# Running the second matmul of a stacked half tile over all 128 rows

## The reference

```python
e = jnp.stack([tbl_0[ids[:, 0]], ..., tbl_38[ids[:, 38]]], axis=1)     # (512, 39, 16)
x0, xk = e, e
for idx, (W, b) in enumerate(params):           # three layers, 128 outputs each
    z = jnp.einsum('bhd,bkd,hks->bsd', x0, xk, W) + b[None, :, None]
    z = jax.nn.relu(z)
    if idx != n_layers - 1:
        xk = z[:, :64, :]
        direct.append(z[:, 64:, :])
    else:
        direct.append(z)
logit = jnp.sum(jnp.concatenate(direct, axis=1), axis=-1)
h = jnp.maximum(jnp.concatenate([logit, dense_ctx], axis=1) @ W_top1 + b_top1, 0.0)
h = jnp.maximum(h @ W_top2 + b_top2, 0.0)
y = h @ W_top3
```

## Time and profile before

| | |
|---|---|
| median of three runs | 661.69 us (661.02 to 662.9) |
| profiled execution | 662.2 us |
| span of its trace | 660.4 us |
| TensorE matmul busy | 623.2 us, 94% |
| VectorE busy | 576.9 us, 87% |
| GpSimd busy | 464.8 us, 70% |
| ScalarE busy | 283.8 us, 43% |
| matmuls at L522 | 32, mean 497 ns |

### The profile page before, as it was taken

The page is one execution under the profiler, slowest core; times in us unless marked ns, Lnnn a source line. Parts: engine busy times, 40 slices in busy tenths (PEclk is TensorE's granted clock), DMA queues, the critical chain, the costliest instruction groups (busy, mean ns, idle before and its releaser), DMA issues.

```text
span 660.4 us, 7186 instructions
## 1 busy us (share of the span) xinstructions
PE 623.2 (94%) x1916; PEld 357.3 (54%) x1916; DVE 576.9 (87%) x507; ACT 283.8 (43%) x341; POOL 464.8 (70%) x277
## 2 busy tenths in 40 slices
PE   0359999999999999999999999999999999999998
PEld 0125555555656555555655555555656555555553
DVE  3358899999999999999999999999999999999670
ACT  2123554444344554444344554444344554444223
POOL 6609877786869877786869877786869877706240
PEclk9998999999999999999999999999999999999999
DMA  6789796877949395967949395967949394962000
GB/s 228 168 201 207 148 211 143 191 148 157 194 109 218 69 223 103 202 136 162 190 109 214 70 222 107 201 137 158 194 111 216 75 227 95 201 132 68 2 0 0
DMA packets 28511, 98.20 MB, mean 149 GB/s; under 512 B 8081, under 2 KB 17041, under 8 KB 20434
## 3 DMA queue, kind: packets, MB, share of 16 engines
q1 hardware_dynamic: 21267, 93.54, 64.1%
q0 software_dynamic: 5120, 1.32, 2.0%
q10 hardware_dynamic: 2111, 3.20, 1.4%
HBM read 94.20 MB, written 3.84 MB: 148 GB/s over the span
## 4 chain that ended last, share of the span: by engine, by line
PE 86%; DVE 5%; issue 4%; ACT 1%; DMA 1%; POOL 1%; SPq 1%; DVEq 0%; POOLq 0%; ACTq 0%
PE z L528 40%; PE z L539 13%; PE z L534 12%; PE z L536 11%; PE z L519 4%; DVE products L406 4%; PE z L522 2%; DMA x_rep<-x_rows 1%; POOL low L309 1%; PE z L521 1%; PE spare L573 1%; PE z L597 1%; DVE low L309 1%; PE xk L597 1%; ACT xk L623 1%
## 5 line engine op out<-in xcount | busy, mean ns | idle before, releaser
L406 DVE TENSOR_TENSOR products<-x_rep,xk 128x1024 f32<-128x1024 f32 (+1 forms) x288 | 366.6, 1333 | 25.5 <-ACT xk L623 25.1
L309 POOL TENSOR_TENSOR low<-products,high 128x1024 fp32r<-128x1024 f32 x112 | 264.9, 2390 | 125.3 <-ACT high L639 83.9
L528 PE MATMUL z<-products,w_whole 128*128 128x512 f32 x672 | 311.2, 595 | 0.0
L639 ACT ACTIVATE high<-products 128x1024 fp32r<-128x1024 f32 x176 | 184.3, 1056 | 237.6 <-DVE products L406 180.5
L362 POOL DMA_INDIRECT gathered<-in_tables,rows_sb x160 | 199.1, 1245 | 46.5 <-issue 44.4
L534 PE MATMUL z<-high,w_high 128*128 128x512 f32 x352 | 187.9, 534 | 10.0 <-ACT high L639 10.0
L528 PEld LDWEIGHTS z<-products,w_whole 128*128 128x128 f32 x672 | 128.1, 191 | 112.0 <-issue 99.1
L536 PE MATMUL z<-high,w_low 128*128 128x512 f32 x352 | 139.7, 397 | 0.0
L539 PE MATMUL z<-low,w_high 128*128 128x512 f32 x352 | 113.9, 405 | 3.0 <-DVE low L309 2.3
L534 PEld LDWEIGHTS z<-high,w_high 128*128 128x128 f32 x352 | 66.8, 190 | 55.5 <-issue 32.9
L309 DVE TENSOR_TENSOR low<-products,high 128x1024 fp32r<-128x1024 f32 x64 | 94.2, 1473 | 1.1 <-ACT high L639 1.1
(11 more groups left out here) (34 smaller groups left out, 102.5 us busy)
## 6 DMA issues: line engine op xcount, KB each, us to landing
x_rep<-x_rows SPq DMA_DIRECT2D x60, 768.0 KB
x_rep<-x_rows SPq DMA_DIRECT2D x62, 512.0 KB, 6.4
x_rows<-gathered SPq DMA_DIRECT2D x15, 225.0 KB
x_rep<-x_rows SPq DMA_DIRECT2D x8, 384.0 KB, 16.0
x_rep<-in_w ACTq DMA_DIRECT2D x2, 1280.0 KB
gathered<-in_tables,rows_sb POOLq DMA_INDIRECT x160
x_same<-x_rows SPq DMA_DIRECT2D x15, 90.0 KB
x_same<-x_rows SPq DMA_DIRECT2D x15, 78.0 KB
```

Of the source, the lines that this page charges most:

```text
L309: ops.tensor_tensor(low[0:p, slot, 0:n, :], products[0:p, index % RING, 0:n, :], high[0:p, slot, 0:n, :].bitcast(fp32), ALU.subtract).then ...
L406: nc.vector.tensor_tensor(slots, rep, row.unsqueeze(1).broadcast_to([p, n, N]), ALU.mult).then_inc(made, 1 + pair)
L528: mm = nc.tensor.matmul(out, w_whole[0:p, at, i, :], products[0:p, slot, i, :], start=(t + i == 0), stop=(t + i == tiles[layer] - 1))
L639: nc.scalar.activation(high[0:p, slot, 0:n, :], products[0:p, index % RING, 0:n, :], ACT.Copy).then_inc(rounded, 1)
```

## The change

The second matmul of a stacked half tile (L522) multiplies all 128 rows of `stacks` by the low part of the weights, where it multiplied rows 0 to 63 before. `w_stack_low` has 128 partitions, with the low part of the same weights in both halves. So the sum gets one more term, the low part of the products by the low part of the weights. The two set-up subtractions (L499) run over 128 partitions.

```diff
-        w_stack_low = sb("w_stack_low", [HALF, len(STACKS), S], fp32r)
+        w_stack_low = sb("w_stack_low", [S, len(STACKS), S], fp32r)
...
-                nc.vector.tensor_tensor(w_stack_low[:, at, :], w_sb[layer][0:HALF, t + 1, :],
-                                        w_stack_high[0:HALF, at, :].bitcast(fp32), ALU.subtract) \
+                nc.vector.tensor_tensor(w_stack_low[:, at, :], w_sb[layer][:, t + 1, :],
+                                        w_stack_high[:, at, :].bitcast(fp32), ALU.subtract) \
                     .then_inc(w_stack_made, 1)
...
-                    mm = nc.tensor.matmul(out, w_stack_low[:, stack, :], stacks[0:HALF, stack, :],
+                    mm = nc.tensor.matmul(out, w_stack_low[:, stack, :], stacks[:, stack, :],
                                           start=False, stop=True)
```

## The result

The changed kernel took 660.36 us, the median of 7 runs (659.28 to 660.51), against 662.60 us (661.02 to 662.95, 7 runs) for the kernel before beside it. The ratio is 0.9968 with a 95% interval of 0.9957 to 0.9978: about 2 us. The median is just over the 0.3% line, which lies inside the interval. Its profiled execution took 660.37 us, with a span of 658.6 us against 660.4.

A forecast was written before the change was run, and what follows sets the result against it. A loop through VectorE, GpSimd, TensorE and ScalarE sets the 37.12 us turn. 15 x 0.115 = 1.7 us plus 0.2 us in the last chunk, off 661.69 us, gives 659.8 us; eight-in-ten range 656.8 to 661.9 us.

The forecast's parts named there:

- The bound: In each turn, TensorE sets the pace only for 9.86 us, from layer 1's fourth group to layer 1's end.
- The rival that it is the bound (649 us): All 32 stacked groups give 0.39 us off TensorE's queue, 649.2 us; chance 0.12 together with half-way cases.
- The spacings: In a stacked group, L521, L522, L534, L536 come 0.64, 0.23, 0.23 us apart, 1.10 us in all for 1.49.
- The rival in which L522 still comes 0.72 us after L521: In stacked groups only the 0.30 us behind L522 goes, landing in the wait: 661.5 us; chance 0.13.
- The tail: Layer 1's stacked group, L522's start to ScalarE's: 0.53 us falls to 0.50, taken as 0.025 us per turn.
- The other end that the prediction named: From L522's start to ScalarE's, the 0.11 us of exposed weight load could vanish in full.
- the last chunk: Final chunk, without layer 0: 0.09 us in layer 1, 0.09 plus 0.03 in layer 2, 0.2 us in all.
- Set-up: Two set-up subtractions over 128 partitions: between nothing and 0.5 us once; nothing was taken.
- slower rival: VectorE's L425 stretches to its maximum beside GpSimd's shifted gathers, 0.33 us more per turn: 664.8 us; chance 0.05.
- the loop: Each turn's chain through VectorE, GpSimd, TensorE and ScalarE, 37.12 us, shortened by 0.115 us per turn; chance 0.70.

The follow-up runs named there:

- the layer 2 kernel: The changed kernel with full rows at L522 in layer 2 alone, layer 1 keeping 64 rows: 661.68 us, ratio 0.9993 to the kernel before.
- the two free matmuls: The changed kernel with two more full-row fp32r matmuls per chunk in layer 2's second group: 661.69 us, ratio 0.9993 to the kernel before.

## Why the prediction was right

**The bound.** Right, and shown by the kernels with one layer changed, with matmuls added and with the order changed. TensorE, busy for 94% of the span, sets the turn only between its second wait for GpSimd and the release of ScalarE. The rival that it is the bound (649 us) fell with the layer 2 kernel and with the two free matmuls.

**The spacings.** 0.64, 0.24, 0.23 us measured for 0.64, 0.23, 0.23 forecast. The rival in which L522 still comes 0.72 us after L521 is out. The Trainium skill ("TensorE: Matmul & The Clock Gate", Part 3, What overlaps and what doesn't), which the prediction cited for it, says that a weight load overlaps a running matmul only when its row group differs. The trace contradicts that sentence: L522's load at 175.57 runs beside L521 on the same 128 rows, 0.23 us ahead of its own matmul. The 0.64 us are no price of going from fp32 to fp32r. L521's record starts 0.02 us behind the second record of L519 (174.71 + 1.02 - 0.59 = 175.14); from there to L522 are 0.66 us, one fp32 spacing of 0.43 us and one fp32r spacing of 0.23 us. With 64 rows it was 0.09 us more.

**The tail was mis-sized.** The step "I take 0.02 to 0.03 us" for the time from L522's start to ScalarE's measured 0.09 us (0.53 to 0.44). It had been read from ScalarE's rounding behind L539, which is a different pair: the kernel puts two waits before that rounding and one before the `relu`, and its L539 had been held by GpSimd. Which of these makes the 0.50 us, no run shows. The other end that the prediction named, the exposed weight load gone in full, was nearly right. So a turn gave 0.18 us and not 0.115. From the first L522 to that of the last chunk, 15 turns, the trace went from 557.31 to 554.64 us: 2.7 us for 1.7 forecast. From there to the last L522 it gave 0.20 us, of which 0.10 us lie behind the first of the two, where the prediction put nothing (0.42 us to the 16-row matmul before, 0.32 us after), and 0.09 us before the second.

**The fall of the clock was not foreseen.** The end is 1.6 us longer than before in the profiled execution (13.73 for 12.13 us). The whole account of the span: 0.6 us less before the first L522 (the start, which has other waits and varies between runs), 2.7 in the turns, 0.2 in the last chunk, 1.6 more in the end, in all 1.8 us, as 660.4 - 658.6. The forecast of -1.9 us came out because 1.0 us more in the turns, 0.6 us at the start and 1.6 us lost at the end nearly cancelled. The mechanism was right; that the sum hit the profiled difference to 0.1 us was luck.

**Set-up and slower rival.** The two subtractions over 128 partitions take 277 to 279 ns, for 274: here twice the partitions cost 3 to 5 ns. L425 of layer 2 took 1.28 us as before in a typical chunk: the loop stayed in step.

## What to carry to other kernels

When an engine is busy for 94% and still waits, however shortly, at a fixed place in each turn, work taken out ahead of that place can be worth nothing, as here: follow the wait back to a loop over the engines, and change what lies between it and the release. To test such a loop, add the same small work on either side of the wait. Removing the waits by an order in which the engine has other work (one string here) took 0.42 us from the turn of the 64-row kernel, where the full-row matmul took 0.18 us, and 1.2% from the time, where it took 0.3%. A 64-row matmul among 128-row ones was no cheaper here than a full one, and made its neighbours wait before and behind it. So fill the rows, or at least put the half-row matmul last, so that the longer spacing behind it falls after the release.

## What the runs showed of the hardware

A 64-row matmul between 128-row ones adds 0.09 us before it (0.72 for 0.64 us), and 0.30 us over the two spacings behind it (0.43 and 0.34 for 0.24 and 0.23 us), and its weight load starts with it and not 0.23 us ahead. At the two waits for GpSimd TensorE's next weight load and matmul start together, and the matmul after it comes 0.34 us later and not 0.23: so each of these waits costs 0.11 us beyond its length. In the dense network at the end, behind matmuls of 32 columns and a wait of 0.49 or 0.69 us, the granted clock fell in some executions (0.61 on average from 646 to 650 us in the changed kernel, so for most of that stretch it was the lower of the two levels, 1.2 and 2.4 GHz) and made the end 1.6 us longer; in others with the same matmuls it stayed at 1.00.
